# Third attention of a fused conv and attention network: its units in another order on every engine

## The reference

```python
t = t + L3_attn(layernorm(t))      # 2 images, 256 tokens each, 8 heads of 16
t = t + L3_ffn(layernorm(t))       # 16 experts, 4 per token, and a shared one

def L3_attn(x):
    local_mask = abs(idx[:, None] - idx[None, :]) > 5
    local_out  = mha(x, l_in_w, l_in_b, l_out_w, l_out_b, mask=local_mask)
    global_out = mha(x, g_in_w, g_in_b, g_out_w, g_out_b)
    x = layernorm(x + local_out + global_out, ln1_g, ln1_b)
    ffn = relu(x @ ffn_w1.T + ffn_b1) @ ffn_w2.T + ffn_b2
    return layernorm(x + ffn, ln2_g, ln2_b)
```

## Time and profile before

| | us |
|---|---|
| median of 3 runs (455.69 to 458.97) | 458.76 |
| the profiled execution | 452.84 |
| its span, from first to last instruction | 450.7 |
| TensorE busy with matmuls in the span | 416.4 (92%) |
| VectorE busy | 216.1 (48%) |
| ScalarE busy | 149.3 (33%) |

### The profile page before, as it was taken

One profiled execution on the slowest core, in us unless ns is written; L12 is line 12 of the kernel. 1 busy time (PEld: TensorE's weight loads), 2 busy tenths in 40 slices (PEclk: granted clock), 3 DMA queues, 4 the chain that ended last, 5 costly groups with the idle time before them and its releaser, 6 DMA issues.

```text
span 450.7 us, 10135 instructions
## 1 busy us (share of the span) xinstructions
PE 416.4 (92%) x3474; PEld 345.4 (77%) x3475; DVE 216.1 (48%) x643; ACT 149.3 (33%) x306; POOL 16.3 (4%) x51
## 2 busy tenths in 40 slices
PE   6789899987678699989999999999999999999996
PEld 3546757755457567534599999999999999999995
DVE  2774564268465254799344334433433343344333
ACT  2400653445563343232222232322322322323231
POOL 7300000000000000110000000000000000000000
PEclk9999999999998889999999999999999999999999
DMA  7200003500000000000550567726771045617250
GB/s 274 104 2 0 1 1 84 196 1 0 1 1 1 1 2 1 1 0 1 188 188 0 180 192 238 261 59 190 259 262 34 17 169 171 201 39 267 66 186 25
DMA packets 32584, 43.58 MB, mean 97 GB/s; under 512 B 1202, under 2 KB 26420, under 8 KB 32436
## 3 DMA queue, kind: packets, MB, share of 16 engines
q1 hardware_dynamic: 32564, 43.31, 29.6%
HBM read 43.05 MB, written 0.26 MB: 96 GB/s over the span
## 4 chain that ended last, share of the span: by engine, by line
PE 83%; DVE 9%; ACT 5%; issue 2%; DMA 1%; SPq 0%; DVEq 0%; ACTq 0%
PE bank L1026 27%; PE bank L1040 14%; PE bank L981 4%; PE bank L702 3%; PE bank L692 3%; PE bank L505 2%; ACT shared_room L1181 2%; PE bank L955 2%; PE bank L782 2%; PE bank L805 2%; PE bank L588 2%; PE bank L945 2%; PE bank L947 2%; PE bank L991 1%; PE bank L996 1%
## 5 line engine op out<-in xcount | busy, mean ns | idle before, releaser
L1026 PE MATMUL bank<-shared_room,w 128*128 128x128 f32 x1100 | 130.9, 275 | 0.0
L1026 PEld LDWEIGHTS bank<-shared_room,w 128*128 128x128 f32 x1100 | 128.7, 192 | 2.7 <-issue 0.5
L1239 ACT ACTIVATE shared_room<-bank 128x512 f32<-128x512 f32 (+1 forms) x75 | 42.1, 562 | 77.8 <-PE bank L1026 77.8
L1763 DVE TENSOR_TENSOR shared_room<-bank,shared_room 128x512 f32<-128x512 f32 (+1 forms) x75 | 48.4, 645 | 39.3 <-PE bank L1026 39.3
L1040 PE MATMUL bank<-w,shared_room 128*128 128x128 f32 (+1 forms) x550 | 66.8, 277 | 0.0
L1040 PEld LDWEIGHTS bank<-w,shared_room 128*128 128x128 f32 (+1 forms) x550 | 63.4, 192 | 0.0
L1771 DVE SCALAR_TENSOR_TENSOR ye_lo<-bank,slot_weight,ye_hi 128x128 fp32r<-128x128 f32 x25 | 8.8, 351 | 71.4 <-ACT ye_hi L1245 71.4
L505 PE MATMUL bank<-ones_bf 128*128 128x512 bf16 x144 | 34.2, 379 | 0.0
L1744 DVE TENSOR_SCALAR pick_bf<-slot_no,place 128x128 bf16 x104 | 22.7, 282 | 23.3 <-issue 23.3
L1063 ACT ACTIVATE spread<-bank 128x512 fp32r<-128x512 f32 x26 | 15.5, 597 | 31.5 <-PE bank L991 31.5
L1245 ACT ACTIVATE ye_hi<-bank,slot_weight 128x128 fp32r<-128x128 f32 x25 | 9.2, 367 | 49.3 <-PE bank L1040 49.3
(11 more groups left out here) (345 smaller groups left out, 491.0 us busy)
## 6 DMA issues: line engine op xcount, KB each, us to landing
w<-in_w SPq DMA_DIRECT2D x34, 682.5 KB, 4.7
w<-in_w SPq DMA_DIRECT2D x17, 640.0 KB
shared_room<-in_experts SPq DMA_DIRECT2D x8, 257.0 KB, 5.8
w<-in_sw SPq DMA_DIRECT2D x2, 682.5 KB, 5.6
l<-in_l SPq DMA_DIRECT2D x1, 1165.0 KB, 9.1
rows<-in_rows SPq DMA_DIRECT2D x1, 780.0 KB, 5.9
w<-in_w SPq DMA_DIRECT2D x17, 42.5 KB
w<-in_sw SPq DMA_DIRECT2D x1, 640.0 KB
```

Of the source, the lines that this page charges most:

```text
L1026: last = mm(bank[b][:, SLOTS * (t - t0):SLOTS * (t - t0 + 1)], w[p][:, 128 * t:128 * t + 128], xe[:, p, :], start=True, stop=True)
L1239: nc.scalar.activation(silu[:, slot, 0:n], bank[slot][:, 0:n], ACT.Silu)\
L1763: tt(he[:, p, t0:t1, :].rearrange("p t s -> p (t s)"), bank[2 + slot][:, 0:n], silu[:, slot, 0:n], ALU.mult).then_inc(sem("he_ready"), 1)
```

## The change

The order becomes a list, `TURNED`, of all that is written to banks 6 and 7: turns, and now the denominators, spreads and projection number 0 to 2 also, which leave banks 4 and 5.

- TensorE: denominators(0) behind unit 4, spread(0) and denominators(1) behind unit 5, spread(1) behind unit 6, projection(0) behind unit 7, denominators(2) behind unit 8, and spread(2) between the two turns of unit 9. Turns, scores and attends keep their places among each other. The attends of image 1 wait for copy_out only.
- VectorE: maxima of u first, then the copy of the last turn of u-1, then divide, invert or add_attention, then the first copies of u. It copies turns 0, 1 and 3 of a global unit and both of a local one. The additions to `u3` move behind its copies of unit 0. It computes the odd half of the global queries, behind its global keys.
- ScalarE: exponentials of u, its copy (turn 2 of a global unit, nothing in a local one), copy_out behind the exponentials at u = 3, 5, 8. Its table load moves ahead of the copy of LN_ATT3's turned y, and one of four query activations is gone.

A line of "..." stands for what is left out.

```diff
@@ -105,8 +105,8 @@
 UNITS_B = len(UNITS) // B
 PARTS = {"g": 4, "e": 1, "l": 4}
 TURNS = {"g": 4, "e": 1, "l": 2}
-BY_ACT = {"g": (3,), "e": (), "l": (1,)}
 ATTENDS = {"g": 2, "e": 1, "l": 2}
+AHEAD = {"g": 3, "e": 1, "l": 1}
 
 
 def total_before(table):
@@ -116,10 +116,36 @@
...
-PART_AT, TURN_AT, ATTEND_AT = total_before(PARTS), total_before(TURNS), total_before(ATTENDS)
-TURN_LIST = [(u, g) for u, (kind, _, _) in enumerate(UNITS) for g in range(TURNS[kind])]
-TURN_BY_ACT = [g in BY_ACT[UNITS[u][0]] for u, g in TURN_LIST]
-TURN_COUNT = [TURN_BY_ACT[:n + 1].count(TURN_BY_ACT[n]) for n in range(len(TURN_LIST))]
+PART_AT, ATTEND_AT = total_before(PARTS), total_before(ATTENDS)
+
+
+DENOMINATORS_AFTER = {UNITS_B - 1: 0, UNITS_B: 1, 2 * UNITS_B - 2: 2}
+SPREAD_AFTER = {UNITS_B: 0, UNITS_B + 1: 1}
+PROJECT_AFTER = UNITS_B + 2
+COPY_OUT_AFTER = {UNITS_B - 2: 0, UNITS_B: 1, 2 * UNITS_B - 2: 2}
+TURNED = []
+for _u, (_kind, _, _) in enumerate(UNITS):
+    TURNED += [("turn", _u, _g) for _g in range(AHEAD[_kind])]
+    if _u == len(UNITS) - 1:
+        TURNED.append(("spread", 2))
+    TURNED += [("turn", _u, _g) for _g in range(AHEAD[_kind], TURNS[_kind])]
+    if _u in SPREAD_AFTER:
+        TURNED.append(("spread", SPREAD_AFTER[_u]))
+    if _u in DENOMINATORS_AFTER:
+        TURNED.append(("denominators", DENOMINATORS_AFTER[_u]))
+    if _u == PROJECT_AFTER:
+        TURNED.append(("project", 0))
+BY_ACT = [_n for _n, _e in enumerate(TURNED) if _e[0] == "turn" and UNITS[_e[1]][0] == "g" and _e[2] == 2]
+TURN_AT = {_e: _n for _n, _e in enumerate(TURNED)}
+
+
+def taken(n):
+
+    return sum((m in BY_ACT) == (n in BY_ACT) for m in range(n + 1))
+
+
+TURN_ORDER = [_e for _e in TURNED if _e[0] == "turn"]
+TURN_SLOT = {_e: _n for _n, _e in enumerate(TURN_ORDER)}
 TURN_SLOTS = 4
 
 
...
+                        pe.wait_ge(sem("q3_odd" if half else "q3_ready"), 1)
                     for r in range(ROWS4):
                         rows4 = slice(32 * r, 32 * r + 32)
                         last = mm(bank[r][:, n * half:n * half + n], q3[s][half][rows4, queries:queries + 128],
...
                 last.then_inc(sem("score3_mm"), 1)
 
-            def wait_copied(n):
-
-                pe.wait_ge(sem("p3T_act" if TURN_BY_ACT[n] else "p3T_dve"), TURN_COUNT[n])
+            def wait_taken(n):
+
+                pe.wait_ge(sem("taken_act" if n in BY_ACT else "taken_dve"), taken(n))
+
+            def room_to_turn(*what):
+
+                n = TURN_AT[what]
+                if n >= 2:
+                    wait_taken(n - 2)
+                return bank[6 + n % 2]
 
             def turn(u, g):
 
                 kind = UNITS[u][0]
...
                 kind, b, t = UNITS[u]
                 for g in ((2 * a, 2 * a + 1) if kind == "g" else (a,)):
-                    wait_copied(TURN_AT[u] + g)
+                    wait_taken(TURN_AT["turn", u, g])
                 if b and kind == "g" and t == 0 and a == 0:
-                    pe.wait_ge(sem("ob3_ready"), 1)
+                    pe.wait_ge(sem("o3_copied"), 1)
                 if b and kind == "e":
-                    pe.wait_ge(sem("u3_added"), 1)
+                    pe.wait_ge(sem("o3_copied"), 2)
...
             def denominators(n):
 
                 pe.wait_ge(sem("o3_copied"), n + 1)
-                if n:
-                    pe.wait_ge(sem("ob3_ready"), n)
+                to = bank[0] if n == 3 else room_to_turn("denominators", n)
...
             def spread_quotients(n):
 
                 pe.wait_ge(sem("rd3_ready"), n + 1)
+                to = bank[0] if n == 3 else room_to_turn("spread", n)
...
             def project(b, s):
 
                 pe.wait_ge(sem("ob3_ready"), 2 * b + s + 1)
+                to = bank[1] if b else bank[6 + TURN_AT["project", 0] % 2]
...
@@ -885,25 +910,26 @@
             local_values()
             pe.wait_ge(sem("v3_ready"), 2)
             for u, (kind, b, _) in enumerate(UNITS):
-                ahead = 3 if kind == "g" else 1
-                for g in range(min(ahead, TURNS[kind])):
+                for g in range(AHEAD[kind]):
                     turn(u, g)
                 if u + 1 < len(UNITS):
                     scores(u + 1)
-                if u in (3, 5, 8):
-                    denominators((3, 5, 8).index(u))
-                if u == 6:
+                else:
+                    spread_quotients(2)
+                if kind == "g":
+                    attend(u, 0)
+                for g in range(AHEAD[kind], TURNS[kind]):
+                    turn(u, g)
+                for a in range(1 if kind == "g" else 0, ATTENDS[kind]):
+                    attend(u, a)
+                if u in SPREAD_AFTER:
+                    spread_quotients(SPREAD_AFTER[u])
+                if u in DENOMINATORS_AFTER:
+                    denominators(DENOMINATORS_AFTER[u])
+                if u == PROJECT_AFTER:
+                    room_to_turn("project", 0)
                     project(0, 0)
                     project(0, 1)
-                attend_first = kind == "g"
-                if attend_first:
-                    attend(u, 0)
-                for g in range(ahead, TURNS[kind]):
-                    turn(u, g)
-                for a in range(1 if attend_first else 0, ATTENDS[kind]):
-                    attend(u, a)
-                if u in (3, 5, 8):
-                    spread_quotients((3, 5, 8).index(u))
             keep_warm(2, WARM_DIVIDE)
             denominators(3)
             project(1, 0)
@@ -1151,16 +1177,16 @@
 
 
             deviation(LN_ATT3)
+            prepare(ACT.Exp)
             ln_copy(LN_ATT3, 2)
 
             def queries(s):
                 act.wait_ge(sem("q3_mm"), s + 1)
-                for half in range(2):
+                for half in range(1 if s == 0 else 2):
                     nc.scalar.activation(q3[s][half][:], bank[4 + 2 * s][:, :], ACT.Identity,
                                          bias=c3("gl"[s] + "_bq")[:, half:half + 1], scale=pair_mask[:, half:half + 1])\
                         .then_inc(sem("q3_ready"), 1)
 
-            prepare(ACT.Exp)
             act.wait_ge(sem("pairs_made"), 1)
             queries(0)
             queries(1)
@@ -1168,7 +1194,7 @@
             def exps(u):
                 kind = UNITS[u][0]
                 if u >= 2:
-                    act.wait_ge(sem("p3T_mm"), TURN_AT[u - 1])
+                    act.wait_ge(sem("p3T_mm"), TURN_SLOT["turn", u - 2, TURNS[UNITS[u - 2][0]] - 1] + 1)
                 if kind == "e":
                     act.wait_ge(sem("nmax3_ready"), PART_AT[u] + 1)
                     nc.scalar.activation(p3[0:EDGE, u % 2, 0, 0:EDGE_K], bank[0][0:EDGE, 0:EDGE_K], ACT.Exp,
...
@@ -1198,11 +1224,11 @@
                 copy(o3[:, n % 2, :], bank[4 + n % 2][:, :]).then_inc(sem("o3_copied"), 1)
 
             for u, (kind, _, _) in enumerate(UNITS):
-                if u in (2, UNITS_B, UNITS_B + 2):
-                    copy_out((2, UNITS_B, UNITS_B + 2).index(u))
                 exps(u)
-                for g in BY_ACT[kind]:
-                    copy_turned(u, g)
+                if kind == "g":
+                    copy_turned(u, 2)
+                if u in COPY_OUT_AFTER:
+                    copy_out(COPY_OUT_AFTER[u])
             copy_out(3)
 
 
@@ -1536,8 +1562,6 @@
             normalise(LN_ATT3, tiles_of(t4))
             dve.wait_ge(sem("y_ready"), NT * turn_of(LN_ATT3) + NT)
 
-            settle(tt(u3[:], y[LN_ATT3][:], row("g_out_b", NT), ALU.add))
-            note(tt(u3[:], u3[:], row("l_out_b", NT), ALU.add))
             dve.wait_ge(sem("l3_in"), 16)
 
             def keys(s):
@@ -1547,6 +1571,8 @@
                     .then_inc(sem("k3_ready"), 1)
 
             keys(0)
+            dve.wait_ge(sem("q3_ready"), 1)
+            ts(q3[0][1][:], bank[4][:, :], pair_mask[:, 1:2], c3("g_bq")[:, 1:2], ALU.mult, ALU.add).then_inc(sem("q3_odd"), 1)
             keys(1)
 
             def values(dst, src, side, n):
@@ -1561,7 +1587,7 @@
 
             def edge_queries():
 
-                dve.wait_ge(sem("q3_ready"), 4)
+                dve.wait_ge(sem("q3_ready"), 3)
                 edge = WINDOWS[1][1]
                 for half in range(2):
                     for b in range(B):
...
             def invert(n):
                 dve.wait_ge(sem("den3_mm"), n + 1)
                 if n:
                     dve.wait_ge(sem("spread3_mm"), n)
-                settle(nc.vector.reciprocal(rd3[:], den_bank(n)[:, 0:16]))
+                found = bank[0] if n == 3 else bank[6 + TURN_AT["denominators", n] % 2]
+                settle(nc.vector.reciprocal(rd3[:], found[:, 0:16]))
+                if n < 3:
+                    dve.sem_inc(sem("taken_dve"), 1)
...
             def divide(n):
                 dve.wait_ge(sem("spread3_mm"), n + 1)
-                tt(ob3[:, n // 2, n % 2, :, :].rearrange("p h q -> p (h q)"), den_bank(n)[:, :], o3[:, n % 2, :], ALU.mult)\
```

(35 more changed lines are left out.)

50 lines of the change are left out of this document (20 added, 30 removed).

## The result

| | before | after |
|---|---|---|
| median of 20 runs, us | 454.87 (452.89 to 459.22) | 459.09 (454.29 to 462.31) |
| ratio, 95% interval | | 1.007 (1.0041 to 1.0098) |

The forecast was +0.8 us and no change that can be told; the medians differ by 4.2 us, and the ratio, which leaves the three slowest of the 20 runs of after out, is some 3.2 us. The change is slower, by less than 1%, and by four to five times what I had forecast. The profiled execution of after took 462.26 us, 3.2 over its median, so its stage shows more half clock than most; the profiled one of before took 452.84, 2.0 under its median, and shows less than most.

What follows compares the result with a forecast made beforehand. A ring through three engines in the third attention was taken to set the pace; waits for VectorE's late copy made 160.8 against 160.0 us at full clock, +0.8, so 459.6 us from the 458.76 median, range 455.0 to 463.5.

Steps and rivals of the forecast that it cites:

- The ring: Third attention: no engine is full; a cycle of waits through three engines sets the pace, with scores 1.07 us.
- What stands ahead of the units: Moved table load, u3 additions and odd half of the queries, before the attention units: 0, between -0.2 and +0.2 us.
- S(5): Moment when the scores of unit 5 are complete: forecast at 128.67 us against 130.05 before.
- The end of the stage: Unit 9: spread waits for the inversion until 157.76 us, VectorE's last copy ends 160.34, last attend 160.8.
- The old order at full clock: Before without its half clock, in the third attention: 4.05 us shorter, old attends ending at 160.0 instead of 164.06 us.
- the 1.38 gained ahead of it: Local units of the first image: unit 5's scores complete 1.38 us earlier, as denominators and spread leave the path.
- I take the same loss in both: Third attention: half clock costs old and new order alike, 4.05 us, as TensorE's work and nearly its idle time stay.
- Rival B: Units 0, 4 and 5: each 2 us wait for VectorE's copy draws another slow stretch; 464.3 us, chance 0.14.
- signs of being wrong: Global units near 5 us from scores to scores; stage clock near 1.00 or under 0.88; first-unit waits from the table load.
- Rivals A and C: A: slow stretches go away, 455.5 us, chance 0.17. C: profile-to-median gap is this stage's slow stretches, and vanishes, 453.6 us, 0.10.
- Rival D: Global units: early exponentials carry through, 4.9 us from scores to scores instead of 6.0; half of it gives 456, chance 0.09.
- The rule on weight loads: Eight attends: loads wait as their matmuls do, 0.65 us each; if loads passed a wait, 0.57 and sum +0.2.

Runs made afterwards that it cites:

- warmed after: After, plus 38 matmuls whose result nobody reads in TensorE's waits ahead of second attends: 452.68 us, ratio 0.9925 to before.
- warmed before: Before, plus 33 matmuls whose result nobody reads in TensorE's waits ahead of first turns and second attends: 449.21 us, ratio 0.9869 to before.
- the side products alone: After with the turned copies placed as in before: 449.3 us, ratio 0.9852; with 16 added matmuls 445.65 us, ratio 0.9786.
- the kernel with the first parts put back: After with the late copy behind the second maximum, and table load, queries and u3 additions placed as in before: 450.07 us, ratio 0.989.
- copies-alone kernel: Before with only the changed copies (VectorE's last one behind the next unit's maxima, ScalarE the third global bank): 471.2 us, ratio 1.0323.

## Why the prediction was right, and where it fell short

**What bounds the stage.** Right. The ring sets the pace, and the wait went from ScalarE's copy to VectorE's: the waits of TensorE ahead of the global attends (2.13, 0.87, 2.08, 0.87 where I had 2.0, 0.75, 2.0, 0.75) and the chain at unit 1 are as forecast, to 0.1 us in each wait.

**What stands ahead of the units.** Right: 0, and 0.04 us measured, within the bounds of 0.2.

**The units, step by step.** The warmed after runs at full clock from S(5) on, so its steps can be laid beside mine: S(5) to S(6) 7.86 us (forecast 7.73), to S(7) 8.25 (8.11), to S(8) 4.94 (5.01), to S(9) 4.09 (3.93). All within 0.2. The waits ahead of the attends, 6.0 and 4.2 us, I had at 5.5 and 5. What isn't seen is S(5) 1.4 us earlier: it is 131.61 there against 130.17 in the warmed before, but behind 7 us of half clock. At 0.35 us each (the fit) to 0.43 (the first slow stretch of before, below) that is worth 2.4 to 3.0 us, so at full clock S(5) would be 1.0 to 1.6 earlier, an estimate that agrees with the forecast without showing it.

**The end of the stage** was a mis-sized term. From S(9) to the last attend I had 7.35 us, and the warmed after takes 8.11. I had the spread wait 0.27 us for the inversion; the profile has 0.8. Chain of waits of after, behind the last denominators:

```profile
167.18 1.00 PE bank L878 x8
168.18 0.02 issue
168.20 0.27 DVE rd L1636
168.47 0.03 issue
168.50 0.02 DVEq L1638
168.52 0.46 issue
168.98 0.44 DVE rd_wide L1639
169.46 1.86 PE bank L887 x8
```

Half a microsecond goes by between the reciprocal and the copy that widens it. Line 1638 is the semaphore increment that the change puts between the two. The same gap is 0.16 us at the first two inversions; what makes it 0.52 at the third I didn't settle. In before, with no increment there, it is 0.03 at all of them, and in three kernels it is 0.16 at the third too: the side products alone, with and without added matmuls, and the kernel with the first parts put back, where the spread waits 0.4 us instead of 0.8. That last one has the late copies, so neither they nor the increment alone make the 0.52, and its cause stays open.

**The old order at full clock.** I took 4.05 us of half clock out of it. The warmed before has 30.25 us from S(5) to the last attend, and I had 29.95: good. Before itself takes 34.00, so half clock cost 3.75 there. The new order has 33.25, and I had 32.13: 1.1 more, 0.8 of it in the end. So from S(5) on the path is 3.0 us longer; less the 1.38 gained ahead of it, which rests on the forecast, that leaves some 1.6 instead of 0.8. Taking 0.35 off for each us of half clock gives 1.7 (445.6 against 447.3), or 1.5 with all 41 runs of before, and 1.8 with the added matmuls. The lines through the runs of each kernel alone cross full clock at 446.7 and 447.3, each uncertain by more than half a microsecond, so 0.8 isn't excluded by them.

**"I take the same loss in both, because TensorE's work is unchanged and its total idle time nearly so."** This is the step that failed. The idle time in sum is nearly the same, but it lies in fewer and longer waits: in 107 to 174 us, 14.2 us in 18 waits in before and 15.1 in 14 in after, and the longest, but for one of 1.7 us that both have, is 1.5 and 2.2. The half clock went from 20.9 us (before, in the later sessions; for the first one only the profiled execution's clock is listed) to 28.3. At 0.35 that is 2.6 us, and with 1.6 of path it makes 4.2. The medians differ by 4.2 within the first session and by 4.0 against the 41 later runs. Rival B had this mechanism with its place, units 0, 4 and 5, and I gave it 0.14. Its price was too high, 4.7 us: it took three stretches of 3.4 us in addition, and 7.4 us of half clock more is nearer to two. The stretches aren't alike either, from 3.4 to 13 us in the profile of after. What the rows said against my step stood in the text: half clock had come behind 2.9 us with TensorE busy for 1.31 of them, and the new order has such a stretch in units 0, 4 and 5. One of my own signs of being wrong came true as well: a stage mean clock under 0.88. It is 0.78 in the profile, and even the median of 28.3 us at half clock, were it all in these 77 us, would make it 0.82. By the same estimate before has 0.86 in its median run; I had set the bound by a profile with 0.93.

**Rivals A and C.** Both were out in the median: no run of after comes near a clock of 1. The best has 0.983 and 452.2 us of span. C rested on the 5.92 us between the profile and the median of three runs; over 20 runs the median of before is 454.87 and the gap is 2.0. The base of my figure was high by chance, by 3.9 us, and the predicted 459.6 lies near the measured 459.09 by luck: that error and the 3.4 us missing from the difference nearly cancel. As a difference the forecast was +0.8 against +4.2.

**Rival D.** Out as it stood: S(1) to S(2) is 6.65 us in after, its last 2.1 at half clock. Yet it is half true. With the copy between the second and third maximum S(1) to S(2) is 4.89 us, where the rival had 4.9 and before has 5.11, and the kernel is as fast as the side products alone (449.08 and 449.3). Whether one copy stood behind four maxima or behind two decided whether the change lost 4 us or gained 7 by the medians (6 by the ratio).

**The rule on weight loads.** The trace agrees with the row and not with a load ahead of a wait. In after the loads of unit 0's second attend begin at 113.86, behind 2.34 us of idling and 0.03 ahead of their matmuls, when VectorE's late copy (113.07 and 0.68) was complete. In the copies-alone kernel it is 113.91 behind 2.34 us.

## What to carry to other kernels

When one engine's queue takes on a copy that another engine waits for, the copy's place among its neighbours counts more than its length: here the four maxima ahead of a 0.69 us copy made the matmul engine wait up to 2.2 us in a unit. Count idle time by the length of each wait and not only in sum, and ask of each long one whether the clock falls behind it. A few matmuls with no reader in waits that can't be removed are cheap to try, and removing one part of a change that has several can show, as here, that one half is a gain and the other a loss.

## What the runs showed of the hardware

- A microsecond at half clock cost some 0.35 us of span in this stage (a line through 20 runs of after; 0.31 through 41 of before; 0.30 to 0.44 where added matmuls changed the clock), and not the 0.5 of an engine that does nothing but its own work. Part of it lies in waits for other engines, which I take to be the reason. Beside the warmed before, the first slow stretch of before (TensorE busy for 3.38 of 3.40 us) cost 1.46 us from S(5) to S(7), so 0.43; I had estimated 1.58.
- The level follows the waits and can be steered by filling them: 33 matmuls in the waits of before raised the mean clock of the stage from 0.93 to 1.00 in the profiled executions and took 5.9 us off, with the order unchanged.
- The same kernel has more or less half clock from run to run: 15 to 38 us in 20 runs of after, with the span 8 us apart. The wait of 1.7 us ahead of the first transposes was followed by half clock in two of 13 profiled executions. One profile says little about such a stage; the clock that each run lists says more.
